# A two-layer graph network on one core: TensorE picks 33 edge tiles of the second layer in place of 36

## The reference, cut to what matters

```
h = relu(layernorm(x));  x = x + attention_layer(h, src, dst)     # first layer
h = relu(layernorm(x))
msg     = h[src] * edge_weight                                     # one row per edge
agg     = segment_sum(msg, dst)                                    # one row per node
h_neigh = agg / max(degree, 1)
out     = x + concatenate([h_neigh, h]) @ W.T + b
```

## Time and profile before

| what | value |
|---|---|
| median of 3 runs | 1577.04 us (1561.55 to 1581.73) |
| profiled execution | 1583.45 us, its span 1581.6 us |
| mean granted clock of TensorE | 0.909 |
| busy share | PE 79%, DVE 68%, ACT 57%, POOL 52% |
| second layer's steps | about 960 to 1577 us of the span |
| GpSimd gathers of the second layer | 380 |
| pick matmuls (L1543) | 900, for 36 tiles |

### The profile page before, as it was taken

How to read it: one execution, slowest core, us unless ns; L and a number is a source line. 1 busy time by engine, 2 the same in 40 slices (tenths; PEclk the granted TensorE clock), 3 DMA queues, 4 the chain that set the end, 5 groups by cost and what they waited for, 6 DMA issues and landing times. The chain is left out here.

```text
span 1581.6 us, 22313 instructions
## 1 busy us (share of the span) xinstructions
PE 1247.6 (79%) x5244; PEld 935.1 (59%) x5244; DVE 1069.3 (68%) x2577; ACT 900.2 (57%) x2624; POOL 830.2 (52%) x863
## 2 busy tenths in 40 slices
PE   6874878878888788888888784588878887888877
PEld 5662666666666566666664462366666666666654
DVE  5761777778787777777877883456666556566656
ACT  2221776677777777767774472355555555455540
POOL 3026255556666656656660206366666566566660
PEclk9986998899999989989998897689999999899998
DMA  6146165556666666656663013133333333233332
GB/s 175 62 136 194 52 166 161 152 161 180 174 168 183 175 177 171 174 151 179 176 175 109 0 54 115 54 90 96 89 93 94 85 96 92 82 94 91 95 89 90
DMA packets 78863, 195.63 MB, mean 124 GB/s; under 512 B 15690, under 2 KB 34674, under 8 KB 78740
## 3 DMA queue, kind: packets, MB, share of 16 engines
q0 software_dynamic: 53952, 169.45, 38.8%
q1 hardware_dynamic: 21278, 21.56, 4.4%
q10 hardware_dynamic: 3510, 3.20, 0.6%
HBM read 180.92 MB, written 13.24 MB: 123 GB/s over the span
## 5 line engine op out<-in xcount | busy, mean ns | idle before, releaser
L734 POOL DMA_INDIRECT ring<-qv_tab,v_src x440 | 434.0, 986 | 368.6 <-PE bank L868 172.0
L1463 POOL DMA_INDIRECT y_ring<-y_tab,e_idx x380 | 371.3, 977 | 298.5 <-PE bank L1562 117.3
L795 ACT ACTIVATE ring<-ring 128x65 f32<-128x65 f32 x1720 | 431.7, 336 | 0.0
L1612 DVE SCALAR_TENSOR_TENSOR kx<-bank,rdeg,kx 128x256 f32 x440 | 212.6, 483 | 244.5 <-PE bank L1562 187.7
L1543 PE MATMUL bank<-y_parts,src_hot 128*128 128x512 f32 x900 | 285.0, 449 | 99.1 <-ACT src_hot L1498 35.2
L854 PE MATMUL bank<-kx,hotT 128*128 x880 | 261.7, 426 | 94.4 <-issue 49.1
L1497 ACT ACTIVATE src_hot<-src_off,piece_id 128x640 fp32r<-128x640 f32 x180 | 149.2, 829 | 259.7 <-PE bank L1543 125.8
L868 PE MATMUL bank<-ring,hot 128*128 128x265 f32 x880 | 280.7, 420 | 8.6 <-issue 5.8
L1562 PE MATMUL bank<-y_ring,hot 128*128 x880 | 252.2, 411 | 35.6 <-SPq L1486 13.4
L854 PEld LDWEIGHTS bank<-kx,hotT 128*128 128x128 f32 x880 | 178.2, 211 | 156.1 <-issue 128.1
L1543 PEld LDWEIGHTS bank<-y_parts,src_hot 128*128 128x128 f32 x900 | 176.6, 201 | 153.5 <-issue 64.8
(11 more groups left out here) (269 smaller groups left out, 984.5 us busy)
## 6 DMA issues: line engine op xcount, KB each, us to landing
ring<-qv_tab,v_src POOLq DMA_INDIRECT x440
qv_tab<-qv_out SPq DMA_DIRECT2D x25, 264.0 KB, 2.0
y_ring<-y_tab,e_idx POOLq DMA_INDIRECT x380
y_tab<-acc SPq DMA_DIRECT2D x12, 256.0 KB, 2.7
out_dram<-kx ACTq DMA_DIRECT2D x24, 128.0 KB
xs<-in_x_dram SPq DMA_DIRECT2D x4, 640.0 KB, 13.3
kx<-in_x_dram SPq DMA_DIRECT2D x4, 640.0 KB
src_i<-in_src_dram SPq DMA_DIRECT2D x36, 64.0 KB
```

The source lines that it names most:

```text
L734: pool.indirect_dma_start(one_step(r, 0, PITCH), None, qv_tab, bass.IndirectOffsetOnAxis(ap=v_src[:, r:r + 1], axis=0)).then_inc(got[r % R ...
L795: A.activation(part, part, ACT.Copy, scale=one_step(r, EX + h, EX + h + 1)).then_inc(scaled, 1)
L1463: pool.indirect_dma_start(y_ring[:, e % RH, :], None, y_tab, bass.IndirectOffsetOnAxis(ap=e_idx[:, e:e + 1], axis=0)).then_inc(y_got[e % R ...
L1612: V.scalar_tensor_tensor(row, bank[r % SB][:, 0:D], rdeg[:, bass.ds(tiles[r % U], 1)], row, ALU.mult, ALU.add).then_inc(sums_added, 1)
```

## The change

The list of tiles that TensorE picks ends earlier. Before it was 27, 38, ..., 412: 36 tiles. Now it is 27, 38, ..., 379: 33 tiles. Tiles 390, 401 and 412 are gathered by GpSimd like their neighbours. Every loop that asks for `BY_PE` follows: the picks, the builds, the readings and loads of src, the copies and adds into the ring, GpSimd's list and the counts for which SyncE waits. The positions of all other instructions relative to the steps stay. ScalarE's loop ends with the copy of tile 379, at step 367, and what follows the loop in its list, the stores, comes next.

```
-        BY_PE = list(range(READ + 2, ET - 2, EVERY))
+        BY_PE = list(range(READ + 2, ET - 3 * EVERY, EVERY))
```

## The result

The kernel with 33 picked tiles takes 1586.18 us (median of 20 runs, 1571.65 to 1597.61), the kernel before 1574.19 us beside it (20 runs, 1561.49 to 1596.98). The ratio is 1.0065, 95% interval 1.0039 to 1.0092: slightly slower, where 1558.7 us and a ratio of 0.9884 had been forecast. (Medians are of all runs; ratios and their intervals leave out runs that fell in a slower state.) Two later comparisons gave 1.0004 (0.9975 to 1.0033) and 1.0014 (0.9976 to 1.0051). So the forecast gain is not there: by these three intervals the change lies between 0.25% faster and 0.9% slower.

What follows compares the result with a forecast made beforehand. TensorE, with its picks, was taken to set the second layer's pace. Without them 51.1 + 1.6 + 4.4 + 3.0 gives 60.1 us instead of 78.5 for steps 368 to 439: 1558.7 us, range 1545 to 1572.

Steps and rivals of the forecast that it cites:

- slow starts and late answers of TensorE: Last term for steps 368 to 439, on top of the 57.1 us bound: 3.0 us, about one low-clock restart.
- the pickless stretch: Steps 400 to 439 before the change: 33.01 us, 0.846 us a step, carried over to all 71 intervals from step 368.
- Rival B: Late answers, not tied to the picks, stay; two of 5 us fall into the stretch; 1568.7 us, chance 0.16.
- C: GpSimd becomes the bound, gathers at 1.61 us after the burst of stores; gain 12.0 us, 1565.1 us, chance 0.06.
- GpSimd's slack: In the second layer GpSimd waits 117.3 us for TensorE, so it was taken to have slack.
- The three gathers cost nothing: Steps on ring tiles already landed hide the three added gathers; without that cover they would cost 3.8 us.
- The arithmetic of landed tiles: Tile 415, needed by step 439 at about 1558.3, is there at 1544.8, 13.5 us ahead.
- The port rule: VectorE can hold a port pair GpSimd needs; a 0.353 us wait per gather would make it 1.61 us, under 1.67.
- packed step: From step 368 VectorE sets the pace, with adds 0.72 us apart where packed, the floor of a step; 51.1 us for 71.
- own adds: VectorE's own-product adds (L1568) at steps 386, 403 and 420: 0.54 us each, 1.6 in all.
- register readings: Reading places and counts into registers at steps 380, 400 and 420: 1.48 us each, 4.4 in all.
- Rival D: TensorE falls to its 1.2 GHz level and stays, 1.22 us a step from step 368; 1591.1 us, chance 0.04.

Runs made afterwards that it cites:

- neither: Changed kernel with tiles 390, 401 and 412 neither picked nor gathered (rows left out); stretch from step 368 to 439 takes 73.51 us.
- drained_6: Changed kernel, stores held back to step 399, GpSimd waiting for its gathers to land after every sixth tile from 382; stretch 59.17 us, ratio 0.9895.
- pool_plain_b: Changed kernel, stores held back, GpSimd issuing plain transfers of 128 neighbouring rows instead of gathers from tile 382, on a chip with late completions; stretch 58.57 us.

## Why the prediction was wrong

**The step that failed** is the last term of the sum, "slow starts and late answers of TensorE", taken over from the pickless stretch after step 400 as 3.0 us. That stretch was no model for steps 368 to 400. It has no picks, but it has hardly any gathers either: the last but one is at 1543.75 in its first moments and the last at 1546.93. I had named it "the pickless stretch" and not asked what else was missing in it. The term measured 77.3 - 57.1 = 20.2 us; it holds the late completions and whatever the lower clock after TensorE's waits added. Without gathers the stretch is 62.8 us, with gathers in runs of six 59.2, so that the term is 5.7 or 2.1 us. There the rest of the sum stands. In one place the term was also misread: of the interval from step 400 to 401 the prediction says that TensorE restarts at the low clock, but the node tile's own product (L1530, L1531) stands in it too, between the two rows:

```profile
1543.27 1.91 PE L1530 MATMUL bank<-w1T,xs 128*128 128x256 f32 x4
```

**Rival B** had the right mechanism and the wrong size: late answers that aren't tied to the picks. I priced them at two waits of 5 us because I had one such row, 4.98 us before step 383. The prediction said that the trace does not tell what was late there. GpSimd's timeline of before tells at least what went with it: ten gathers in a row had ended at 1517.5, and GpSimd was released within 0.1 us of VectorE's add at 1519.67.

```profile
1519.77 0.95 POOL L1463 DMA_INDIRECT y_ring<-y_tab,e_idx  x1 [2.24 <-remote]
```

The range reached to 1572 for it and C, and the time lay beyond. By and large the lateness grows with the length of GpSimd's runs: 2.5 us with runs of up to 7, 4.2 to 6.4 with 8 to 10, 9.6 to 11.9 with 15 to 17, with `neither` as the exception (5.7 at 14). Taking picks away lengthens the runs: 10 gathers at most in a row in this stretch before, 15 after. So the change itself brought back the cost whose absence it counted on, which a price taken from the old trace does not show. Before the change GpSimd's wait for a ring slot breaks the runs. With steps of 0.85 us and gathers of 1.26 it would hardly wait, as I wrote, and I booked this as free.

**GpSimd's slack.** "The three gathers cost nothing" does not hold: without them the stretch is 3.8 us shorter (neither, 73.51 us, one execution against one). The arithmetic of landed tiles was right all the same. With ScalarE's loads at a higher rate 60.64 us were reached.

**The port rule.** Gathers took 32.50 us for 34 beside VectorE, 0.96 each, so the wait for VectorE that the Trainium skill's page "SBUF — State Buffer" (section "Who interferes with whom") makes possible was not seen here. Whether L1573 ever ran in that mode no run here shows. The same section says that "PE and ACT never wait on anyone". TensorE's records themselves agree, with 22 of them in 8.38 us beside gathers; its completions nevertheless reach the others up to 11.9 us late in these stretches. Whether a port has any part in that is not shown.

**What held:** 0.72 us a packed step (drained_6 has long rows of them), and the prices of own adds and register readings. Rival D did not decide: the granted clock did fall to 0.81 in the first window, where TensorE waits, but once the late completions were gone (drained_6 at 0.96, pool_plain_b at 0.97) the stretch took 58.6 to 59.2 us.

**What stays open.** First, how the gathers hold TensorE's completions. Shown is that it takes indexed gathers of GpSimd (not traffic, bytes, busyness or the semaphore wait), that it is small when the runs are kept to six, and that it ends some 1 to 2 us after GpSimd stops. The path in the chip is not. All of it is read from executions that the profiler recorded; whether the completions are as late without it, no run shows. Second, why one chip of those used has none of it. Third, the 0.65% of the first comparison: the stretch of the change is 1.2 us shorter in the profiled executions, not longer, and the time of steps 0 to 368, where the programs are the same, ran from 524 to 541 us over the profiled kernels on the chips with late completions. I can't place 0.65% in that.

## What to carry over

When a stretch of the trace is to stand for what another will be after a change, list all that is absent from it, not only what the change takes away. And when steps of one engine come back late with a releaser that the profile can't name, look at which other engine stops just before each release: here the pairs stood in the trace of before already. With long runs of GpSimd gathers broken by a short wait for their landing, and the stores held back, the changed kernel took 1.05% less than the kernel before on a chip where completions are late. On the chip where they are not, pauses after every eighth tile cost 0.56%.

## What the runs showed of the hardware

TensorE's completions can lag far behind its records while GpSimd issues indexed gathers. In the changed kernel's second layer 158 of the 340 increments that the trace holds for the step sums come over 0.1 us after the latest end of a step; of those that VectorE and ScalarE make there, none comes more than 0.02 us after an instruction's end. The clearest case is in the trace of the kernel before, at the start of the second layer, where it could have been read beforehand (TensorE, VectorE, GpSimd):

```profile
978.79 1.02 PE L1562 MATMUL bank<-y_ring,hot 128*128 x4
1001.29 2.50 PE L1543 MATMUL bank<-y_parts,src_hot 128*128 128x512 f32 x5 [21.48 <-issue]
...
988.39 0.48 DVE L1612 SCALAR_TENSOR_TENSOR kx<-bank,rdeg,kx 128x256 f32 x1 [10.29 <-remote]
...
1005.23 0.48 DVE L1612 SCALAR_TENSOR_TENSOR kx<-bank,rdeg,kx 128x256 f32 x1 [15.88 <-PE bank L1562]
...
954.77 0.99 POOL L1463 DMA_INDIRECT y_ring<-y_tab,e_idx  x1 [76.69 <-POOLq L1149]
...
1002.22 0.95 POOL L1463 DMA_INDIRECT y_ring<-y_tab,e_idx  x1 [0.31 <-issue]
```

37 gathers in a row, 954.77 to 1003.18, and TensorE's steps 11 to 13, recorded before 980, reach VectorE from 1005 on; that of step 11 is 28.4 us late. Steps 0 to 20 take 58.5 us here, and 26.5 to 28.0 on the chip without lateness, where GpSimd issues the same gathers. Pauses in this run of gathers were not tried.

Chips differ by much more than the changes that are compared on them: the same kernel before took 1546 to 1577 us (medians) on four of the chips and 1296 us on a fifth, where the mean granted clock of the profiled kernels was 0.96 to 0.97 in place of 0.90 to 0.92 and the steps 0 to 368 took 420 to 422 us in place of 524 to 541.
